# Heads projected in full fp32 with whole output weights, row maxima of two slots in one transpose, and a new order of work within a step, in a two-layer PixArt transformer kernel

## The chip, the cores and the metric

The kernel runs on one core of one Trainium2 chip. The metric is the device time of one execution in microseconds (us); the kernel before stands at 1827.0 us, the median of three runs. The engines of the core are named as the profile names them: PE is TensorE's matmuls and PEld its weight loads, DVE is VectorE, ACT is ScalarE, POOL is GpSimd, SP is SyncE, which here only issues DMAs.

## What is computed

32 sequences of 128 tokens and 256 features pass through two transformer layers in fp32. Both have self-attention, cross-attention against a context of 128 tokens, and an MLP of width 1024, with 16 heads of 16 features. They differ in the modulation, in the gates (layer 0) and in the rotary embedding of queries and keys (layer 1).

```python
# layer 0 (biases left out); layer 1 has rope on q and k, no gates, and a norm before cross-attention too
q, k, v = split(modulate(ln(x)) @ qkv_w)
attn = softmax(q @ k.T * SCALE) @ v             # 16 heads of 16
x = x + gate_sa * (attn @ sa_proj_w)
x = x + cross_attention(ln(x), context) @ ca_proj_w
x = x + gate_ff * (gelu(modulate(ln(x)) @ fc1_w) @ fc2_w)
```

## The kernel before, in words

The 32 sequences are cut into 8 groups of 4 (GB = 4). With two layers there are 16 group passes (groups 0 to 7 are layer 0, groups 8 to 15 layer 1), and each pass has 8 batches: 4 sequences in self-attention (s = SELF), then the same 4 in cross-attention (s = CROSS). All engines run the same written-out schedule. Time is cut into steps; group g starts at step 26 g (PERIOD = 26), self-attention at its step 0, cross-attention at its step 16 (CROSS_FROM), and the MLP of a group is done from its step 36 on (MLP_FROM), that is in steps 10 to 17 of the next group. A step is no fixed time: it is a position in the instruction lists. Tables give the step of each stage (AT_TURN_MAX = 2 means two steps after a batch's first scores), and within a step each engine goes through its stages in a fixed order. Every engine works through its own list in order, and semaphores alone tie the lists together, so a wait at the head of one engine's list holds all that stands behind it.

What a batch passes through, with its place in steps after its start:

- Steps 0 and 1: two rounds of scores on PE (L594), each for two of four row groups, into the two banks `score0` and `score1`. DVE takes the row maxima of each bank with a TENSOR_REDUCE (L1040, `row_max`). The next round may overwrite the banks only when both maxima are made.
- Step 2: PE transposes the maxima (`turn_max`, L639), four 128x128 transposes, and DVE adds them to the transposed queries (`less_max`, L1050), so that the exponent needs no subtraction.
- Steps 3 and 4: the transposed scores (L614), interleaved with the score round of a later batch; ACT takes the exponents (L903, L905).
- Step 6: probabilities times values (`mix_values`, L650); ACT copies the result (L912). Step 7: four transposes back to tokens (`turn_heads`, L658); at step 8 DVE divides by the sum (`scale_heads`, L1056 and L1060) and PE transposes the heads (`turn_back`, L665).
- The heads are then split into a high and a low part for the fp32r product: ACT casts `heads_hi` (L918, step 8), DVE subtracts `heads_lo` (L1065, first in step 9), and PE projects in step 9 (`project`, L488 to L490): six fp32r matmuls of 128x256 for two row tiles, low times high, high times low, high times high. DVE takes the result (L1078 in layer 1, L1082 in layer 0).
- Steps 10 and 11: moments, normalisation (`normalise`, L1005) and the transposes of the normalised rows (`turn_z`, L521), modulated on ACT (L824, L829) into `xt_hi`, with `xt_lo` made on POOL.

The projections of queries, keys and values are called units: twelve fp32r matmuls each into the bank `p_unit`, at the steps of the table UNIT_AT. The projection of the heads uses the same bank. In layer 0, keys leave the bank through ACT (L875, half of the heads) and then DVE (L1012, the other half). In layer 1, queries and keys leave it through ACT (L866), are swapped on DVE (L1025), and rotated on POOL by three products and sums of 1.3 us (L1288, L1291, L1294).

The MLP goes through four hidden tiles at a time (`up`, `down`), six fp32r matmuls each, with the Gelu on ACT and the split of the hidden tile on DVE (L1089, L1091).

## Time and profile before

| what | value |
|---|---|
| median of three runs | 1827.0 us (1824.12 to 1827.39) |
| the profiled execution | 1822.23 us, span 1820.4 us |
| mean granted TensorE clock | 0.967 of full speed |
| PE busy | 1595.2 us, 88% |
| PEld busy | 1390.5 us, 76% |
| DVE busy | 1142.6 us, 63% |
| ACT busy | 970.2 us, 53% |
| POOL busy | 726.6 us, 40% |
| DMA | mean 27 GB/s |

The span is the time from the first to the last recorded instruction on the core; the execution's own time is 1.8 us more. A PE matmul's duration includes its way through the array, and matmuls overlap, so the cost of one in a row of them is the distance from start to start, not its duration. One group period (26 steps) takes 106 to 109 us.

### The profile page before, as it was taken

The numbers are of one execution on the slowest core, as the hardware profiler recorded it, in microseconds if no ns is written. First come the engines' busy times: TensorE is split into PE (matmuls) and PEld (weight loads), VectorE is DVE, ScalarE is ACT, GpSimd is POOL, SyncE is SP. The second block draws the span as 40 slices with busy tenths as digits, with TensorE's granted clock in tenths as the row PEclk, the third lists the DMA queues.
The fourth block names the chain that finished last, engine by engine and source line by source line (L and its number), as shares of the span: only waits on it lengthen the run. The fifth ranks groups of instructions, "written<-read, shape, count | busy, mean of one in ns | idle before, by whom it ended". The sixth has DMA issues, their size and how long they took to land.

```text
span 1820.4 us, 46362 instructions
## 1 busy us (share of the span) xinstructions
PE 1595.2 (88%) x18272; PEld 1390.5 (76%) x18272; DVE 1142.6 (63%) x2630; ACT 970.2 (53%) x2011; POOL 726.6 (40%) x983
## 2 busy tenths in 40 slices
PE   5779989898998989989897898989989898988987
PEld 4657878787887877878787787877878787787866
DVE  3446656566665656657667766666766666676654
ACT  2446455555545656455664545646465564545533
POOL 1332424224142332424536546364454536546321
PEclk9989999999999999999999999999999999999989
DMA  6010010101001010011111100000000000000000
GB/s 218 16 46 2 14 48 14 49 8 43 14 15 48 12 51 3 13 48 33 45 36 30 36 13 25 10 20 12 10 25 13 25 7 19 14 13 13 2 13 13
DMA packets 33972, 49.50 MB, mean 27 GB/s; under 512 B 3456, under 2 KB 24896, under 8 KB 33760
## 3 DMA queue, kind: packets, MB, share of 16 engines
q1 hardware_dynamic: 33760, 46.54, 8.3%
q8 instruction: 149, 2.44, 0.6%
q14 instruction: 63, 0.52, 0.1%
HBM read 38.07 MB, written 8.45 MB: 26 GB/s over the span
## 4 chain that ended last, share of the span: by engine, by line
PE 68%; DVE 14%; issue 8%; ACT 7%; POOL 2%; DMA 0%; SPq 0%; DVEq 0%; ACTq 0%; POOLq 0%
PE score L594 8%; PE p_unit L488 7%; PE score_t L614 7%; PE p_mix L650 5%; PE p_unit L490 5%; PE p_unit L489 5%; DVE neg_max L1040 5%; PE p_out L488 4%; PE p_out L489 3%; PE p_out L490 3%; PE p_turn L639 3%; PE p_turn L665 2%; PE p_turn L658 2%; PE p_mix L521 2%; ACT xt L824 2%
## 5 line engine op out<-in xcount | busy, mean ns | idle before, releaser
L1040 DVE TENSOR_REDUCE neg_max<-score 128x4 f32<-128x512 f32 x512 | 329.9, 687 | 209.8 <-PE score L594 208.9
L594 PE MATMUL score<-k_t,q_t 32*128 32x256 f32 x2048 | 303.1, 415 | 63.9 <-issue 18.3
L614 PE MATMUL score_t<-q_less,k_t 32*128 32x128 f32 x4096 | 313.2, 293 | 0.7 <-ACT probs_t L905 0.7
L594 PEld LDWEIGHTS score<-k_t,q_t 32*128 32x128 f32 x2048 | 192.8, 195 | 111.9 <-issue 56.2
L905 ACT ACTIVATE probs_t<-score_t 128x512 f32<-128x512 f32 x384 | 209.1, 599 | 120.8 <-PE score_t L614 120.6
L614 PEld LDWEIGHTS score_t<-q_less,k_t 32*128 32x128 f32 x4096 | 262.9, 196 | 13.3 <-issue 9.2
L824 ACT ACTIVATE xt<-p_mix,mod_now 128x128 f32<-128x128 f32 x384 | 154.7, 456 | 161.9 <-PE p_mix L521 132.1
L1247 POOL TENSOR_TENSOR xt_lo<-xt,xt_hi 128x256 fp32r<-128x256 f32 x128 | 93.4, 729 | 356.0 <-ACT xt_hi L829 356.0
L488 PE MATMUL p_out<-w_hi,hid_lo 128*128 128x256 f32 x512 | 148.1, 289 | 3.4 <-DVE hid_lo L1091 2.8
L1089 DVE CAST hid_hi<-hid 128x256 fp32r<-128x256 f32 x256 | 94.5, 369 | 83.1 <-ACT hid L891 82.8
L1091 DVE TENSOR_TENSOR hid_lo<-hid,hid_hi 128x256 fp32r<-128x256 f32 x256 | 138.5, 541 | 8.8
L490 PE MATMUL p_out<-w_hi,hid_hi 128*128 128x256 f32 x512 | 143.6, 280 | 0.0
L489 PE MATMUL p_out<-w_lo,hid_hi 128*128 128x256 f32 x512 | 143.4, 280 | 0.0
L650 PE MATMUL p_mix<-probs_t,v_pad 128*32 128x128 f32 x4096 | 139.2, 277 | 1.1 <-ACT xt L824 1.1
L488 PE MATMUL p_unit<-w_hi,heads_lo 128*128 128x256 f32 x256 | 82.8, 323 | 64.9 <-ACT heads_hi L918 33.9
L488 PE MATMUL p_unit<-xt_hi,w_lo 128*128 128x256 f32 x384 | 123.0, 320 | 18.8 <-ACT q_t L870 5.9
L918 ACT CAST heads_hi<-p_turn 128x256 fp32r<-128x256 f32 x128 | 47.6, 372 | 167.3 <-PE p_turn L665 166.7
L891 ACT ACTIVATE hid<-score,bias_cols 128x256 f32<-128x256 f32 x128 | 60.4, 474 | 133.2 <-PE score L490 125.2
L1065 DVE TENSOR_TENSOR heads_lo<-p_turn,heads_hi 128x256 fp32r<-128x256 f32 x128 | 54.2, 423 | 106.1 <-ACT heads_hi L918 106.0
L650 PEld LDWEIGHTS p_mix<-probs_t,v_pad 128*32 128x32 f32 x4096 | 104.6, 110 | 21.1 <-issue 13.1
L1240 POOL TENSOR_TENSOR rstd<-var_eps,minus_half 128x1 f32<-128x1 f32 x192 | 110.2, 574 | 15.0
L488 PEld LDWEIGHTS p_unit<-w_hi,heads_lo 128*128 128x128 f32 x256 | 47.9, 187 | 89.2 <-ACT heads_hi L918 53.1
(151 smaller groups left out, 4525.7 us busy)
## 6 DMA issues: line engine op xcount, KB each, us to landing
ctxt<-in_ctxT SPq DMA_DIRECT2D x16, 512.0 KB, 3.7
side<-gates SPq DMA_DIRECT2D x15, 512.0 KB, 5.6
x_new<-in_x SPq DMA_DIRECT2D x32, 128.0 KB, 2.0
x_mid<-xs SPq DMA_DIRECT2D x8, 512.0 KB, 3.4
x_new<-x_mid SPq DMA_DIRECT2D x32, 128.0 KB, 2.0
out<-xs SPq DMA_DIRECT2D x8, 512.0 KB, 2.9
k_t<-in_L_f_wT SPq DMA_DIRECT2D x2, 1024.0 KB, 5.7
k_t<-in_ln_wT SPq DMA_DIRECT2D x2, 512.0 KB, 7.9
```

The source lines that it names most:

```text
L488: pe.matmul(dst, lhs[1], rhs[0], start=first, stop=False, skip_group_check=shared)
L489: pe.matmul(dst, lhs[0], rhs[1], start=False, stop=False, skip_group_check=shared)
L490: return pe.matmul(dst, lhs[0], rhs[0], start=False, stop=last, skip_group_check=shared)
L594: mm = pe.matmul(score[r % 2][:, t * 2 * N:(t + 1) * 2 * N].rearrange("p (e n) -> p e n", e=2), q_t[s][rows(r), t, tokens], k_t[s][rows(r) ...
L614: mm = pe.matmul(score_t[r % 2][:, x * N:(x + 1) * N], k_t[s][rows(r), t, e, tokens], q_less[rows(r), j % 2, t, e, :], start=True, stop=True)
L650: mm = pe.matmul(p_mix[rows(r), x * N:(x + 1) * N], v_pad[s][:, b, at:at + 32], probs_t[j % 2][:, r, x, :], start=True, stop=True, tile_po ...
L824: op = act.activation(xt[:, k, c, :], p_mix[:, c * P:(c + 1) * P], ACT.Identity, scale=mod_now[k][:, c, b:b + 1], bias=mod_now[k][:, 2 + c ...
L905: op = act.activation(dst, score_t[r % 2][:], ACT.Exp)
L1040: dve.tensor_reduce(by_half[:, :, 2 * r + 1:2 * r + 9:7, 0], score[r % 2][:].rearrange("p (t e n) -> p t e n", t=CT, e=2), AX.X, ALU.max, ...
L1089: dve.tensor_copy(hid_hi[:, u % HID_SLOTS, :], hid[:, u % 2, :]).then_inc(hid_hi_made, 1)
L1091: dve.tensor_tensor(hid_lo[:, u % HID_SLOTS, :], hid[:, u % 2, :], hid_hi[:, u % HID_SLOTS, :].bitcast(F32), ALU.subtract).then_inc(hid_lo ...
L1240: pool.tensor_tensor(rstd[:, k, b:b + 1], var_eps[:, k, b:b + 1], minus_half[:], ALU.pow)\
```

## The change

Four things change.

1. **The heads' projection.** The output weights of self- and cross-attention leave the table of split weights (`w_hi`, `w_lo`) and stand whole in a tile `w_out`, loaded by their own DMAs. ACT copies the transposed heads to `heads_t` in fp32 (one COPY in the place of the cast), the subtraction on DVE (`low_heads`) is gone, and `project` is two fp32 matmuls of 128x256 in the place of six fp32r ones.
2. **Maxima of two slots share one transpose.** The maxima of the two heads of a slot pair are written into one 128-column tile; `turn_max` is two transposes in the place of four, and `less_max` is two SCALAR_TENSOR_TENSOR on 128x256 elements (one for each of the pair, with the column `one_row` as a factor that picks the row) in the place of one TENSOR_TENSOR on 128x512. The two heads of a pair change places in the layout (`by_slot`, `head_mask`, `one_row`).
3. **Tables.** First-norm transposes and units move by a step or two (FIRST_LNT, UNIT_AT), two MLP hidden tiles move between steps, the last `down` stands two steps later.
4. **Order within a step.** On each engine some stages change places.

The core of the diff:

```diff
-FIRST_STATS, FIRST_Z, FIRST_LNT = -13, -11, -10
+FIRST_STATS, FIRST_Z, FIRST_LNT = -13, -9, -9
-UNIT_AT = {-7: ("k", SELF, 0), ...
-           6: ("k", CROSS, 0), 7: ("v", CROSS, 0), 13: ("k", CROSS, 1), 14: ("q", CROSS, 0), 15: ("v", CROSS, 1), 18: ("q", CROSS, 1)}
+UNIT_AT = {-6: ("k", SELF, 0), ...
+           6: ("k", CROSS, 0), 7: ("v", CROSS, 0), 11: ("k", CROSS, 1), 14: ("q", CROSS, 0), 16: ("v", CROSS, 1), 18: ("q", CROSS, 1)}
-for _step, _n in zip(range(MLP_FROM, MLP_FROM + 8), (0, 9, 2, 1, 5, 11, 3, 1)):
+for _step, _n in zip(range(MLP_FROM, MLP_FROM + 10), (0, 10, 1, 1, 6, 12, 1, 0, 0, 1)):
-PE_ORDER = ("round", "proj", "max", "mlp", "norm", "mix", "turn", "first", "unit", "back")
+PE_ORDER = ("round", "proj", "mlp", "max", "mix", "turn", "norm", "first", "unit", "back")
+        w_out = sb("w_out", [P, 2, CT, D])
-        heads_hi = sb("heads_hi", [P, CT, N], F32R)
-        heads_lo = sb("heads_lo", [P, CT, N], F32R)
+        heads_t = sb("heads_t", [P, CT, N])
             def turn_max(group, j):
...
-                for x in range(SLOTS):
-                    mm = pe.transpose(p_turn[:, x * P:(x + 1) * P], neg_max[:, j % 2, x * P:(x + 1) * P], ident[:])
+                for t in range(CT):
+                    mm = pe.transpose(p_turn[:, t * P:(t + 1) * P], neg_max[:, j % 2, t, :], ident[:])
             def project(group, s, b):
...
                 for t in range(CT):
-                    mm = product(p_unit[:, 0:D], (heads_hi[:, t, :], heads_lo[:, t, :]),
-                                 w(W_SA if s == SELF else W_CA, t, D, 0, D), t == 0, t == CT - 1)
+                    mm = pe.matmul(p_unit[:, 0:D], heads_t[:, t, :], w_out[:, s, t, :], start=(t == 0), stop=(t == CT - 1))
-            def high_heads(group, j):
+            def move_heads(group, j):
...
-                act.copy(heads_hi[:].rearrange("p t n -> p (t n)"), p_turn[:, 0:D]).then_inc(heads_hi_made, 1)
+                act.copy(heads_t[:].rearrange("p t n -> p (t n)"), p_turn[:, 0:D]).then_inc(heads_moved, 1)
             def less_max(group, s, b):
...
-                own = q_t[s][:, :, b * N:(b + 1) * N].unsqueeze(2).broadcast_to([P, CT, 2, N])
-                dve.tensor_tensor(q_less[:, j % 2], p_turn[:].rearrange("p (t e n) -> p t e n", t=CT, e=2), own, ALU.add)\
-                   .then_inc(queries_less, 1)
+                for e in range(2):
+                    op = dve.scalar_tensor_tensor(q_less[:, j % 2, :, e, :],
+                                                  p_turn[:, 0:CT * N].rearrange("p (t n) -> p t n", t=CT),
+                                                  one_row[:, e:e + 1], q_t[s][:, :, b * N:(b + 1) * N],
+                                                  ALU.mult, ALU.add)
+                op.then_inc(queries_less, 1)
-            def low_heads(group, j):
-                dve.wait_ge(heads_hi_made, group * 8 + j + 1)
-                dve.tensor_tensor(heads_lo[:].rearrange("p t n -> p (t n)"), p_turn[:, 0:D],
-                                  heads_hi[:].rearrange("p t n -> p (t n)").bitcast(F32), ALU.subtract)\
-                   .then_inc(heads_lo_made, 1)
```

Line numbers in the rows below are those of the kernel before or after, as each list says.

**DVE, group 12 (layer 1), from the end of step 2 to step 3.** Before, from `less_max` of one batch to the result of the projection (L1078):

```order
L1050 TENSOR_TENSOR q_less<-p_turn,q_t 128x512 [waits scored_t,max_turned]
L1025 STREAM_SHUFFLE side<-side 128x512 [waits raw_made]
L1065 TENSOR_TENSOR heads_lo<-p_turn,heads_hi 128x256 [waits heads_hi_made]
L1005 TENSOR_SCALAR z<-xs,mean_var,rstd 128x256 [waits z_turned2,rstd_made2]
L1040 TENSOR_REDUCE neg_max<-score 128x2x2 [waits scored] x2
L1078 TENSOR_TENSOR xs<-p_unit,xs 128x256 [waits projected]
```

And in the changed kernel:

```order
L1055 SCALAR_TENSOR_TENSOR q_less<-p_turn,one_row,q_t 128x2x128 [waits scored_t,max_turned]
L1055 SCALAR_TENSOR_TENSOR q_less<-p_turn,one_row,q_t 128x2x128
L1030 STREAM_SHUFFLE side<-side 128x512 [waits raw_made]
L1010 TENSOR_SCALAR z<-xs,mean_var,rstd 128x256 [waits z_turned2,rstd_made2]
L1045 TENSOR_REDUCE neg_max<-score 128x2x2 [waits scored] x2
L1080 TENSOR_TENSOR xs<-p_unit,xs 128x256 [waits projected]
```

The subtraction that waits for ACT is gone from the head of the step, and the rest keeps its order.

**PE, group 4 (layer 0), from step 20 to step 21.** Before, the transposes of the maxima end step 20, and the round of step 21 (mask, scores, transposed scores) and the unit of the next group's self queries follow:

```order
L639 MATMUL p_turn<-ident,neg_max 128x128 [waits queries_less,max_made]
L639 MATMUL p_turn<-ident,neg_max 128x128 x3
L589 MATMUL score<-mask_row,ones_row 128x512 [waits max_made]
L589 MATMUL score<-mask_row,ones_row 128x512
L594 MATMUL score<-k_t,q_t 128x256 [waits exps_made,queries_less]
L594 MATMUL score<-k_t,q_t 128x256
L614 MATMUL score_t<-q_less,k_t 128x128 x4
L594 MATMUL score<-k_t,q_t 128x256 x2
L614 MATMUL score_t<-q_less,k_t 128x128 x4
L488 MATMUL p_unit<-xt_hi,w_lo 128x256 [waits keys_high,xt_lo_made0,xt_hi_made0]
```

In the changed kernel, from the same transposes on:

```order
L651 MATMUL p_turn<-ident,neg_max 128x128 [waits queries_less,max_made]
L651 MATMUL p_turn<-ident,neg_max 128x128
L533 MATMUL p_mix<-ident,z 128x128 [waits ln_moved0,z_made0]
L533 MATMUL p_mix<-ident,z 128x128
L500 MATMUL p_unit<-xt_hi,w_lo 128x256 [waits queries_made,xt_lo_made0,xt_hi_made0]
L501 MATMUL p_unit<-xt_lo,w_hi 128x256
L502 MATMUL p_unit<-xt_hi,w_hi 128x256
```

Between the transposes and the round of step 21 stand now the last first-norm transpose and the unit of the self keys (12 matmuls), which stood in step 19 before; the unit of the queries keeps its place behind the round, and still waits until the keys have left the bank (`keys_high`). Step 19 gets the last `down` of the MLP, from step 17.

**ACT, group 12 (layer 1), steps 18 and 19.** Before: `modulate` of the third sequence of the next group's first norm (L824 twice, L829) waits for the unit in step 18 (`unit_full`), and the copy of that unit (L866, cross queries) comes behind it:

```order
L882 ACTIVATE k_t<-side,one_row,head_mask 128x2x256 [waits keys_summed]
L824 ACTIVATE xt<-p_mix,mod_now 128x128 [waits unit_full,xt_lo_made0,z_turned0]
L824 ACTIVATE xt<-p_mix,mod_now 128x128
L829 CAST xt_hi<-xt 128x2x128 [waits ln_moved0]
L866 ACTIVATE side<-p_unit 128x512 [waits queries_made,queries_less,unit_full]
L905 ACT_TABLE_LOAD [waits mixed]
```

In the changed kernel:

```order
L833 ACTIVATE xt<-p_mix,mod_now 128x128 [waits xt_lo_made0,z_turned0]
L833 ACTIVATE xt<-p_mix,mod_now 128x128
L838 CAST xt_hi<-xt 128x2x128 [waits ln_moved0]
L875 ACTIVATE side<-p_unit 128x512 [waits queries_made,queries_less,unit_full]
L914 ACT_TABLE_LOAD [waits mixed]
```

The sequence modulated ahead of the copy is now the second one, which doesn't wait for the unit; the third comes behind the exponents of step 19.

## Rows read from the trace of the kernel before

**Rows 1.** The page, busy time of the engines: us, share of the span, instructions

```profile
PE 1595.2 (88%) x18272; PEld 1390.5 (76%) x18272; DVE 1142.6 (63%) x2630; ACT 970.2 (53%) x2011; POOL 726.6 (40%) x983
```

**Rows 2.** The page, the chain that ended last, by engine

```profile
PE 68%; DVE 14%; issue 8%; ACT 7%; POOL 2%; DMA 0%; SPq 0%; DVEq 0%; ACTq 0%; POOLq 0%
```

**Rows 3.** Timeline of PE in group 12, step 3: start, us, what

```profile
1356.38 0.36 PE L488 MATMUL p_unit<-w_hi,heads_lo 128*128 128x256 f32 x1 [0.49 <-ACT v_pad L855]
...
1357.17 0.38 PE L521 MATMUL p_mix<-ident,z 128*128 128x128 f32 x2
1357.38 0.60 PE L658 MATMUL p_turn<-ident,mix_sb 128*128 128x128 f32 x4
1358.41 0.48 PE L594 MATMUL score<-k_t,q_t 32*128 32x256 f32 x2 [0.43 <-DVE neg_max L1040]
```

**Rows 4.** Timeline of PE at the start, the bias products in fp32

```profile
36.69 1.16 PE L794 MATMUL score_t<-probs_t,hid 128*128 128x256 f32 x4
```

**Rows 5.** Line L794, durations of one in ns, least, median and most

```profile
L794 PEld LDWEIGHTS score_t<-probs_t,hid x4: 190/254/337, 36.3 to 37.3; 128*128 128x128 f32 x4
L794 PE MATMUL score_t<-probs_t,hid x4: 379/380/507, 36.7 to 37.5; 128*128 128x256 f32 x4
```

**Rows 6.** Timeline of all engines, group 12, from step 10 to step 11

```profile
1379.71 0.44 PE L665 MATMUL p_turn<-ident,heads 128*128 128x128 f32 x2
1380.19 0.37 ACT L918 CAST heads_hi<-p_turn 128x256 fp32r<-128x256 f32 x1 [0.30 <-PE p_turn L665]
...
1380.59 0.42 DVE L1065 TENSOR_TENSOR heads_lo<-p_turn,heads_hi 128x256 fp32r<-128x256 f32 x1 [1.06 <-ACT heads_hi L918]
...
1381.12 0.36 PE L488 MATMUL p_unit<-w_hi,heads_lo 128*128 128x256 f32 x1 [0.97 <-ACT heads_hi L918]
```

**Rows 7.** Waits of PE's weight loads: us in total, times, longest

```profile
PEld p_unit L488 <- ACT heads_hi L918: 53.1, 43, 1.5
PEld score L594 <- DVE neg_max L1040: 36.4, 48, 3.6
```

**Rows 8.** Timeline of DVE in group 12, step 3

```profile
1355.23 0.42 DVE L1065 TENSOR_TENSOR heads_lo<-p_turn,heads_hi 128x256 fp32r<-128x256 f32 x1 [1.29 <-ACT heads_hi L918]
1355.57 1.28 DVE L1005 TENSOR_SCALAR z<-xs,mean_var,rstd 128x256 f32<-128x256 f32 x1
1356.78 1.28 DVE L1040 TENSOR_REDUCE neg_max<-score 128x4 f32<-128x512 f32 x2
```

**Rows 9.** Timeline of all engines in group 4 (layer 0), step 20

```profile
560.27 0.99 DVE L1012 TENSOR_SCALAR k_t<-p_unit,head_mask,key_bias 128x256 f32<-128x256 f32 x2 [4.26 <-ACT k_t L875]
561.18 1.28 DVE L1040 TENSOR_REDUCE neg_max<-score 128x4 f32<-128x512 f32 x2
...
562.52 0.58 PE L589 MATMUL score<-mask_row,ones_row 32*128 32x512 bf16 x2 [2.43 <-DVE neg_max L1040]
```

**Rows 10.** Timeline of all engines in group 12 (layer 1), steps 19 and 20

```profile
1425.24 0.81 ACT L824 ACTIVATE xt<-p_mix,mod_now 128x128 f32<-128x128 f32 x2 [1.42 <-PE p_unit L490]
...
1426.38 0.59 ACT L866 ACTIVATE side<-p_unit 128x512 f32<-128x512 f32 x1
...
1427.24 1.30 POOL L1288 TENSOR_TENSOR q_t<-side,cos_t 128x512 f32<-128x512 f32 x1
...
1431.38 0.48 PE L594 MATMUL score<-k_t,q_t 32*128 32x256 f32 x2 [2.60 <-issue]
```

**Rows 11.** Windows of groups 11 and 12: stretch, engines' busy time, PEclk

```profile
1236.60:1343.00 106.40, 94.81 (x1133) 83.13 (x1132) 73.04 (x168) 59.10 (x123) 53.71 (x66) 1.00 0.05 16
1343.00:1451.50 108.50, 97.10 (x1130) 85.22 (x1130) 72.75 (x168) 59.10 (x123) 53.64 (x66) 0.97 0.05 16
```

**Rows 12.** Line L1050 (less_max), durations of one in ns

```profile
L1050 DVE TENSOR_TENSOR q_less<-p_turn,q_t x128: 681/682/692, 59.9 to 1769.4; 128x512 f32<-128x512 f32 x128
```

**Rows 13.** Line L1005 (normalise) in group 12, durations of one in ns

```profile
L1005 DVE TENSOR_SCALAR z<-xs,mean_var,rstd x8: 403/407/1281, 1346.3 to 1417.1; 128x256 f32<-128x256 f32 x8
```

**Rows 14.** Window of one period of layer 0, group 2, as in rows 11

```profile
253.70:362.50 108.80, 98.87 (x1144) 85.83 (x1141) 66.60 (x157) 60.30 (x127) 35.16 (x57) 0.97 0.09 26
```

More of the change, by code:

```diff
@@ L258, in build_blocks @@
                  k_t[1][:].rearrange("p t e n -> p (t e n)")]
+        stage = [spare[c][:, 0:CHUNKS[c + 1] - CHUNKS[c]] for c in range(4)]
+        new_stage = [spare[c % 2 * 3][:, 0:CHUNKS[c + 1] - CHUNKS[c]] for c in range(4)]
         ada = [xs[:].rearrange("p a b c -> p (a b c)")[:, 0:6 * D],
@@ L469, in body @@
                             load_weights(1, CHUNK_AT[group, step], new_stage, w_new)
+                        if (group, step) in HEADS_OUT_AT:
+                            s = HEADS_OUT_AT[group, step]
+                            sp.wait_ge(projected, NG * 8 - 4 if s == SELF else NG * 8)
+                            load_heads_out(1, s)
                         if step == LAST:
@@ L753, in body @@
                             turn_heads(group, 4 * s + b)
+                    for group, step in live(t):
+                        for s, b in batch_at(step, AT_LNT):
+                            turn_z(group, s + 1, b)
                     for group, step in live(t):
@@ L953, in body @@
                     for group, step in live(t):
+                        if layer_of(group) == 1 and step in KEYS_AT:
+                            low_keys(group, KEYS_AT[step])
+                    for group, step in live(t):
+                        for n in GELU_AT.get(step, ()):
+                            gelu(group, n)
+                    for group, step in live(t):
                         for s, b, h in round_at(step, AT_EXP):
@@ L969, in body @@
                     for group, step in live(t):
-                        if layer_of(group) == 1 and step in KEYS_AT:
-                            low_keys(group, KEYS_AT[step])
+                        for s, b in batch_at(step, AT_MIX + ACT_MIX):
+                            move_mix(group, 4 * s + b)
                     for group, step in live(t):
@@ L1140, in body @@
                     for group, step in live(t):
-                        for s, b in batch_at(step, AT_TURN_BACK + DVE_LOW):
-                            low_heads(group, 4 * s + b)
+                        for k, b in normed_at(step, AT_Z, FIRST_Z):
+                            normalise(group, k, b)
                     for group, step in live(t):
@@ L1148, in body @@
                             moments(group, k, b)
-                    for group, step in live(t):
-                        for k, b in normed_at(step, AT_Z, FIRST_Z):
-                            normalise(group, k, b)
                     for group, step in live(t):
@@ L1159, in body @@
                     for group, step in live(t):
-                        for s, b in batch_at(step, AT_TURN_MAX):
-                            less_max(group, s, b)
-                    for group, step in live(t):
-                        if layer_of(group) == 1 and UNIT_AT.get(step - DVE_SWAP, "v")[0] != "v":
-                            swap(group, UNIT_AT[step - DVE_SWAP])
-                    for group, step in live(t):
                         for s, b in batch_at(step, AT_PROJ + DVE_OUT):
@@ L1170, in body @@
                             high_keys(group, KEYS_AT[step])
+                    for group, step in live(t):
+                        for s, b in batch_at(step, AT_TURN_MAX):
+                            less_max(group, s, b)
                     for group, step in live(t):
@@ L1178, in body @@
                             make_masks(group)
+                    for group, step in live(t):
+                        if layer_of(group) == 1 and UNIT_AT.get(step - DVE_SWAP, "v")[0] != "v":
+                            swap(group, UNIT_AT[step - DVE_SWAP])
                     for group, step in live(t):
@@ L1314, in body @@
                     for group, step in live(t):
+                        for s, b in batch_at(step, AT_PROJ + DVE_OUT):
+                            if layer_of(group) == 0:
+                                add_output(group, 4 * s + b)
+                    for group, step in live(t):
                         for k, b in normed_at(step, AT_LNT + ACT_MOD, FIRST_LNT + ACT_MOD):
```

149 lines of the change are left out of this document (67 added, 82 removed).

## Prediction

> **What bounds the kernel now.** I read the busy times first: PE is at work 88% of the span, DVE 63%, ACT 53%, POOL 40% [rows 1]. The chain that ended last says the same of the path: 68% of it is PE, DVE has 14%, ACT 7%, and 8% is issue [rows 2]. So work taken from PE should count nearly in full, except in steps whose length is set by a wait. I then read the timeline of two layer-1 steps and one of layer 0 for those waits. Three kinds matter.
>
> First, in steps 11, 13 and 15 nothing stands between the transpose of the heads and their projection: PE transposes at 1379.71, ACT casts at 1380.19, DVE subtracts at 1380.59, and PE begins at 1381.12 [rows 6]. PE's weight loads wait 53.1 us in all for this, 43 times [rows 7].
>
> Second, a score round may start only when both maxima of the round before are made. Rounds wait 36.4 us for that [rows 7]. In step 3 of group 12 the round waits until 1358.41 [rows 3], since on DVE `heads_lo` had waited for ACT with everything behind it, then `normalise` took 1.28 us, and the maxima began only at 1356.78 [rows 8].
>
> Third, the joints around step 20. In layer 0 the self keys leave their bank through ACT and then DVE ahead of the maxima, and the next round stands idle for 2.43 us [rows 9]. In layer 1 the rotation of the last cross queries is late: ACT copies them at 1426.38, POOL starts at 1427.24, and the round that needs them starts at 1431.38 after 2.60 us of idling [rows 10].
>
> **The change part by part.** The sum is made against the profiled execution, 1822.2 us, which is 4.8 us under the median. There are 128 batches and 16 group passes.
>
> *Projection.* Six fp32r matmuls take 0.79 us from the first start to the next stage (1356.38 to 1357.17) [rows 3], 0.13 us each. Two fp32 matmuls of 128x256 are seen at the start: four of them take 1.16 us to the end of the last, which itself lasts 0.38, so three distances make 0.78 us, 0.26 each [rows 4, 5]. The longest of them lasts 507 ns against 379, so it ran in part at the lower clock; if the whole first distance was doubled, d = 0.78/4 = 0.195. I take 0.22, between. A projection is then 0.44 us, and saves 0.35: 128 x 0.35 = 45 us (34 with 0.26, 51 with 0.195).
>
> The weight side could speak against this. The fp32 load of 128 columns has 190 ns as its least duration [rows 5], and it is inside the distance above, so no further price is due. The Trainium skill, TensorE: Matmul & The Clock Gate, in the section on Fast Weight Load, says that the fast load is on for 128 weights only where the type is not FP32; by that rule heads and weights kept in full precision would lose it, and this trace shows no separate price of that. What it would make is the second rival.
>
> *Transposes.* Four transposes last 0.60 us and two 0.38 [rows 3]: two fewer are 0.22 us. 128 x 0.22 = 28 us, hidden nowhere, since PE is the engine at work; in a step that waits anyway it is worth nothing.
>
> *The subtraction on DVE, as a link.* From its start at 1380.59 to PE's start at 1381.12 is 0.53 us; without it PE could start about 0.1 us after ACT's end at 1380.56, 0.45 us sooner [rows 6]. Three places a group: 48 x 0.45 = 22 us (0 if something else is late, 27 from the whole distance and more in step 15).
>
> *The subtraction on DVE, as a block.* In steps 1, 3 and 5 it stood ahead of `normalise` and the maxima. What is won is bounded by the 36.4 us of rounds that wait for maxima [rows 7], part of which stays at step 20. In step 3 of group 12 the projection would still begin at 1356.38, since it waits there for ACT's `v_pad`; with 0.44 for it, and 0.22 and 0.44 for the transposes behind it, the round could start at 1357.5 in place of 1358.41 [rows 3], 0.9 us, of which 0.35 is counted. I take half of the bound, 18 us (0 to 36).
>
> *Step 20, layer 0.* One first-norm transpose pair and the unit of the self keys (twelve matmuls of 0.12 us) now fill the wait of 2.43 us. But the same keys leave the bank one step later: what takes from 560.27 to the maxima's end [rows 9] now stands ahead of the maxima of step 21, beside that step's round. The wait moves and shrinks; I take 1.2 us x 8 = 10 us (0 to 19).
>
> *Steps 19 and 20, layer 1.* The copy of the cross queries no longer stands behind `modulate`, which starts at 1425.24, as the copy could; at most 1.14 us [rows 10]. The swap on DVE still stands behind two maxima, so I take 0.6 x 8 = 5 us. The last `down` (six matmuls, 0.7 us) moves from step 17 into this wait of 2.60 us and so is free: 6 us. Together 11 (0 to 15).
>
> *Clock.* One period of layer 1 at a granted clock of 1.00 takes 106.4 us and the next, at 0.97, 108.5 [rows 11]; a stretch at 1.2 GHz in a period thus costs 2.1 us. Layer 0 has it too, 0.97 [rows 14], behind the long idling of step 20. That idling shrinks in layer 0 (I take half of 8 x 2.1, 8 us) and may lengthen in layer 1, which loses up to 4 x 2.1 (I take 4). Net 4 us (-8 to 17).
>
> *less_max.* Two operations on 128x256 elements, of which the nearest row is `heads_lo`: it reads the same two memories, lasts 0.42 us and lets the next start 0.34 later [rows 8]. Twice 0.34 to 0.42 stands against one of 0.68 [rows 12]: 0 to 0.16 us more, 20 us in all at most. Behind the transposes PE has other work in nearly every step (values, a unit), which covers it; where the cover is gone the next round is late by the whole of it. I take 3 us.
>
> *Covered at nothing:* ACT's copy in place of its cast (same size), the smaller weight splits at the change of layers, two more DMAs of the output weights on SP's queue, which wait for projections long done, and the store two steps later, which the next write to its tile follows by four steps.
>
> Sum: 45 + 28 + 22 + 18 + 10 + 11 + 4 - 3 = 135 us. Not all of it adds up, because a shorter PE step meets DVE, whose even steps hold division, moments, maxima and `less_max`. I hold back 10 us for these new waits: 125. 1822.2 - 125 = 1697, and 1702 at the level of the median.
>
> **The rivals.**
>
> *Only the work counts (15%).* DVE and ACT keep the pace in the rounds, so the second kind of wait and the joints stay, and a quarter of the saved PE work falls into waits: 0.75 x 73 + 11 for half of the link = 66 us, giving 1761. For it: 14% of the chain is DVE's [rows 2]. Against it: DVE loses an operation of 0.42 us a batch and stands idle 1.29 us ahead of the very one that is removed [rows 8].
>
> *The fp32 product is dearer in place (6%).* If each of its two loads stays exposed, 2 x 0.19 us come on top [rows 5], and the projection takes 0.82: nothing is saved on it, 45 us less, 1747. This is the case that the skill's rule on fast loads would make; the distance of rows 4, which holds four loads, speaks against it.
>
> *Everything adds up (14%).* No holding back, all joints at their upper bounds and no stretch at 1.2 GHz in layer 0: 125 + 10 + 9 + 4 + 13 + 5 = 166 us, 1661.
>
> *Slower (4%).* `less_max` might be held by POOL as `normalise` is: that one lasts 407 ns in the median and 1281 at most [rows 13], 0.87 more. 256 halves at 0.87 are 223 us, and the change loses from 144 held halves on (125/0.87); all of them held gives 1702 + 223 = 1925. Against it: L1050, with the same operands, never lasts over 692 ns in 128 [rows 12]. The Trainium skill, SBUF — State Buffer, section Who interferes with whom, says that a DVE instruction with at most one SBUF input outside the two-port modes does not contend with GpSimd; by that rule, and `q_t` is the one tensor here from SBUF, the trace of L1050 agrees.
>
> **How the numbers follow.** The forecast has 61%, with its own range of 1675 to 1735. 1650 to 1765 takes in both neighbours and the dearer product, and leaves out the slower case and what lies beyond: under 2 in 10. About 0.2% (4 us) is what a measurement here can tell from no change. Faster by more: 0.61 + 0.15 + 0.06 + 0.14 = 0.96, of which I move 0.02 to no change, for the first rival carried on until the waits take all; slower 0.04.
>
> **What would show it.** In the profile after: 256 fp32 matmuls into `p_unit` about 0.22 us apart; three projections a group that wait under 0.8 us for ACT; no DVE row ahead of `normalise` that waits for ACT; the wait ahead of layer 0's round of step 21 gone and a smaller one in step 21 on `keys_high`; PE's busy time down by some 70 us; periods of about 100 us in layer 0 and layer 1. I am wrong if PE's idle time grows by as much as its work falls, if the rounds wait more for maxima than 36 us, or if the granted clock falls below 0.96.

## The result, and the profile after

The changed kernel takes 1799.2 us (median of 4 runs, 1797.4 to 1803.8) against 1825.6 (4 runs, 1823.4 to 1827.4) for the kernel before on the same chip: ratio 0.986, 95% interval 0.9836 to 0.9884. It is faster, by 26 us; the forecast was 125 us, and the time lies far above its range of 1650 to 1765. The profiled execution took 1797.4 us with a mean granted clock of 0.959 (0.967 before).

The page of the changed kernel (busy time, then the chain that ended last):

```profile
PE 1594.9 (89%) x17760; PEld 1372.3 (76%) x17760; DVE 1117.6 (62%) x2628; ACT 972.2 (54%) x2009; POOL 720.3 (40%) x983
...
PE 74%; DVE 8%; ACT 8%; issue 6%; POOL 3%; DMA 1%; SPq 0%; DVEq 0%; ACTq 0%; POOLq 0%
```

This is already half of the answer. PE was to lose some 70 us of work and lost 0.3 us [rows 1]. Its share of the chain grew from 68 to 74% while DVE's fell from 14 to 8% [rows 2]: waits for DVE were taken out, but PE's own work did not shrink. The count of matmul records shows why. Before to after, 768 fp32r products go, 256 transposes go, and 256 fp32 products come: 768 fewer. The page has 512 fewer. Line L687, the new projection, in the view of one line (durations in ns, least, median, most):

```profile
L687 PEld LDWEIGHTS p_unit<-w_out,heads_t x512: 186/190/337, 87.5 to 1760.2; 128*128 128x128 f32 x171
L687 PE MATMUL p_unit<-w_out,heads_t x512: 379/379/765, 87.5 to 1760.4; 128*128 128x256 f32 x171
```

256 instructions are 512 records: each fp32 product is recorded as two matmuls, and each of them has its own weight load. The four records of [rows 4] that priced it were two instructions (the line of the bias products issues four in all, and the trace of before has eight records of it). Group 12, step 3, timeline of PE, the place of [rows 3]:

```profile
1339.20 1.10 PE L687 MATMUL p_unit<-w_out,heads_t 128*128 128x256 f32 x4 [0.49 <-ACT v_pad L864]
1340.13 0.60 PE L670 MATMUL p_turn<-ident,mix_sb 128*128 128x128 f32 x4
1340.57 0.38 PE L533 MATMUL p_mix<-ident,z 128*128 128x128 f32 x2
1340.88 0.48 PE L606 MATMUL score<-k_t,q_t 32*128 32x256 f32 x2
```

The projection takes 0.93 us to the start of the next stage, where the six split products took 0.79. The round starts 1.68 us behind the projection's start; before, it was 2.03, of which 0.43 was idling for `neg_max`. That idling is gone, and 0.14 of the gain is paid to the product. What was right in kind: the link without the subtraction, here from step 10 to step 11 of group 12 (all engines; [rows 6] before):

```profile
1362.21 0.44 PE L677 MATMUL p_turn<-ident,heads 128*128 128x128 f32 x2
1362.68 0.37 ACT L927 COPY heads_t<-p_turn 128x256 f32<-128x256 f32 x1 [0.30 <-PE p_turn L677]
1363.11 1.13 PE L687 MATMUL p_unit<-w_out,heads_t 128*128 128x256 f32 x4 [0.46 <-ACT heads_t L927]
```

From transpose to product it is now 0.90 us, before 1.41: 0.51 less, as forecast (0.45).

The waits of PE and of its weight loads (us in total, times, longest):

```profile
PEld p_unit L687 <- ACT heads_t L927: 47.2, 51, 1.7
PEld score L606 <- DVE neg_max L1045: 29.8, 42, 2.3
PE p_unit L500 <- DVE k_t L1017: 18.5, 16, 2.3
PE score L606 <- POOL q_t L1293: 30.8, 8, 4.3
PE p_turn L677 <- DVE q_less L1055: 12.7, 22, 0.9
```

The last two have grown. The rotated queries keep one round of each layer-1 period waiting, 30.8 us in all; the same eight rounds waited 25.0 us before (2.59 or 2.60 us in six of them, as in [rows 10]). And the transposes that turn the heads back wait for `less_max` 22 times, 12.7 us, where they waited 8 times, 2.2 us: both use `p_turn`, and `less_max` has become longer. Its line, and the place in group 12 on PE (maxima turned, last product of the values, then the wait):

```profile
L1055 DVE SCALAR_TENSOR_TENSOR q_less<-p_turn,one_row,q_t x256: 463/475/485, 63.6 to 1745.0; 128x256 f32<-128x256 f32 x128
```

```profile
1341.99 0.44 PE L651 MATMUL p_turn<-ident,neg_max 128*128 128x128 f32 x2
...
1343.57 0.28 PE L502 MATMUL p_unit<-w_hi,xt_hi 128*128 128x256 f32 x1
1344.29 0.41 PE L677 MATMUL p_turn<-ident,heads 128*128 128x128 f32 x2 [0.44 <-DVE q_less L1055]
```

Steps 18 to 20 of a layer-1 period, all engines:

```profile
1403.97 0.56 PE L500 MATMUL p_unit<-xt_hi,w_lo 128*128 128x256 f32 x1
...
1406.77 0.60 ACT L875 ACTIVATE side<-p_unit 128x512 f32<-128x512 f32 x1 [1.17 <-PE p_unit L502]
...
1407.44 1.28 POOL L1287 TENSOR_TENSOR q_t<-side,cos_t 128x512 f32<-128x512 f32 x1 [1.03 <-ACT side L875]
...
1407.83 1.29 DVE L1045 TENSOR_REDUCE neg_max<-score 128x4 f32<-128x512 f32 x2 [2.13 <-PE score L606]
...
1409.04 0.72 DVE L1030 STREAM_SHUFFLE side<-side 128x512 f32<-128x512 f32 x1
...
1411.25 1.26 POOL L1293 TENSOR_TENSOR q_t<-q_t,side 128x512 f32<-128x512 f32 x1
...
1412.72 0.48 PE L606 MATMUL score<-k_t,q_t 32*128 32x256 f32 x2 [3.76 <-POOL q_t L1293]
```

ACT copies the unit at once, as forecast, and POOL starts at once. But the shuffle on DVE stands behind two maxima and ends at 1409.76, and the rest of the rotation on POOL follows from that. The round waits 3.76 us where it waited 2.60 [rows 10]. The unit ahead of it, from 1403.97, has products 0.21 us apart where 0.12 is usual. The windows say why (one period each, from about step 3 of groups 3, 10, 11 and 12; then the unit's stretch alone; the last columns are PEclk, DMA share, GB/s):

```profile
370.30:476.10 105.80, 96.83 (x1114) 83.17 (x1113) 66.55 (x158) 60.52 (x127) 34.88 (x57) 0.98 0.09 27
1122.30:1228.50 106.20, 97.12 (x1098) 84.08 (x1098) 71.56 (x168) 59.39 (x123) 53.61 (x65) 0.97 0.06 17
1228.50:1336.90 108.40, 99.42 (x1099) 86.24 (x1098) 70.61 (x168) 59.38 (x123) 53.47 (x65) 0.94 0.05 16
1336.90:1443.00 106.10, 97.16 (x1099) 84.45 (x1098) 70.63 (x168) 59.44 (x123) 53.53 (x65) 0.97 0.05 17
1402.10:1406.70 4.60, 4.60 (x29) 4.02 (x28) 2.40 (x5) 2.42 (x6) 2.19 (x3) 0.63 0.00 0
```

Most of that stretch ran at 1.2 GHz, one of the clock's two levels. No period of layer 1 shown here is free of it, where group 11 was before, at 1.00 and 106.4 us [rows 11]. A period of layer 0 is 105.8 us, 3 us shorter [rows 14]; these three of layer 1 are 106.9 on average, against 107.5 for the two of [rows 11].

### The profile page after: what moved, and what is told of

The parts are those of the page before. It is cut to its first block, busy times and chain, and to the rows that moved or that the text cites. A ratio compares the mean times of both kernels' runs of the same rounds, so it can differ in the third digit from the quotient of the medians.

```text
span 1795.6 us, 45329 instructions
## 1 busy us (share of the span) xinstructions
PE 1594.9 (89%) x17760; PEld 1372.3 (76%) x17760; DVE 1117.6 (62%) x2628; ACT 972.2 (54%) x2009; POOL 720.3 (40%) x983
## 4 chain that ended last, share of the span: by engine, by line
PE 74%; DVE 8%; ACT 8%; issue 6%; POOL 3%; DMA 1%; SPq 0%; DVEq 0%; ACTq 0%; POOLq 0%
PE score L606 9%; PE p_unit L687 8%; PE score_t L626 7%; PE p_unit L500 6%; PE p_mix L662 5%; PE p_unit L501 5%; PE p_unit L502 5%; PE p_out L500 3%; PE p_out L502 3%; PE p_out L501 3%; DVE neg_max L1045 3%; PE p_turn L670 2%; PE p_mix L533 2%; PE p_turn L677 2%; PE p_turn L651 2%
## 5 line engine op out<-in xcount | busy, mean ns | idle before, releaser
L606 PE MATMUL score<-k_t,q_t 32*128 32x256 f32 x2048 | 303.9, 416 | 65.5 <-POOL q_t L1293 30.8
L626 PE MATMUL score_t<-q_less,k_t 32*128 32x128 f32 x4096 | 307.0, 289 | 0.8 <-ACT probs_t L914 0.8
L626 PEld LDWEIGHTS score_t<-q_less,k_t 32*128 32x128 f32 x4096 | 257.1, 192 | 13.3 <-issue 9.2
L914 ACT ACTIVATE probs_t<-score_t 128x512 f32<-128x512 f32 x384 | 209.1, 598 | 106.2 <-PE score_t L626 105.8
L687 PE MATMUL p_unit<-w_out,heads_t 128*128 128x256 f32 x512 | 144.3, 404 | 42.8 <-ACT heads_t L927 15.8
L1091 DVE CAST hid_hi<-hid 128x256 fp32r<-128x256 f32 x256 | 102.0, 398 | 81.6 <-ACT hid L900 80.8
L500 PE MATMUL p_out<-w_hi,hid_lo 128*128 128x256 f32 x512 | 149.1, 291 | 1.5 <-DVE hid_lo L1093 0.3
L687 PEld LDWEIGHTS p_unit<-w_out,heads_t 128*128 128x128 f32 x512 | 87.2, 190 | 75.1 <-ACT heads_t L927 47.2
L500 PE MATMUL p_unit<-xt_hi,w_lo 128*128 128x256 f32 x384 | 126.1, 328 | 20.6 <-DVE k_t L1017 15.6
L927 ACT COPY heads_t<-p_turn 128x256 f32<-128x256 f32 x128 | 47.7, 372 | 154.5 <-PE p_turn L677 154.1
L1055 DVE SCALAR_TENSOR_TENSOR q_less<-p_turn,one_row,q_t 128x256 f32<-128x256 f32 x256 | 111.2, 476 | 28.2 <-PE p_turn L651 28.2
L501 PE MATMUL p_unit<-xt_lo,w_hi 128*128 128x256 f32 x384 | 117.6, 306 | 0.0
```

Of the source, the lines that this page charges most:

```text
L500: pe.matmul(dst, lhs[1], rhs[0], start=first, stop=False, skip_group_check=shared)
L501: pe.matmul(dst, lhs[0], rhs[1], start=False, stop=False, skip_group_check=shared)
L606: mm = pe.matmul(score[r % 2][:, t * 2 * N:(t + 1) * 2 * N].rearrange("p (e n) -> p e n", e=2), q_t[s][rows(r), t, tokens], k_t[s][rows(r) ...
L626: mm = pe.matmul(score_t[r % 2][:, x * N:(x + 1) * N], k_t[s][rows(r), t, e, tokens], q_less[rows(r), j % 2, t, e, :], start=True, stop=True)
L687: mm = pe.matmul(p_unit[:, 0:D], heads_t[:, t, :], w_out[:, s, t, :], start=(t == 0), stop=(t == CT - 1))
L914: op = act.activation(dst, score_t[r % 2][:], ACT.Exp)
```

## The experiments

Each kernel was timed against the kernel before on the same chip. "Busy" kernels have filler: superfluous transposes of the identity into an unused quarter of a bank, at places where PE waits. They change no result.

### One part alone: projection, maxima, order

e1 is the kernel before with part 1 of the change alone, e2 with part 2 alone, e3 with parts 3 and 4 alone; e4 is the changed kernel with the split projection put back, that is parts 2 to 4. Their diffs are the pieces shown under the change. The kernel before had medians of 1822.9 to 1825.6 us in the different series of runs, so a difference between two kernels of different series is uncertain by a few us; the ratios are each within one series.

> The kernel before with the projection alone changed (whole fp32 weights, two fp32 matmuls for six fp32r, no subtraction on DVE). Theory 1: an fp32 product of 128x256 is worked as two passes of 0.216 us, so a projection costs 0.97 us in place of 0.79 (128 x 0.18 = 23 us lost), and the link without DVE gives back some 16 to 25 us: ratio 0.995 to 1.005. Theory 2 (the product costs 0.44 us as forecast, and new waits eat the gain elsewhere): the projection's own distance to the next stage is 0.44 us and the ratio is 0.98 or lower.

> The kernel before with the shared transposes of the maxima alone. Theory 1: 0.22 us less PE work in each of 128 batches counts nearly in full, 20 to 28 us, ratio 0.985 to 0.989. Theory 2 (waits of the rounds for DVE take it): under 8 us, ratio over 0.995.

> The kernel before with the new tables and the new order within a step alone. Theory 1: the joints around step 20 gain 1 to 2 us in a period of layer 0 and about nothing in layer 1, start-up loses some: 5 to 15 us, ratio 0.992 to 0.997. Theory 2 (the new order moves waits into worse places): slower, ratio 1.002 to 1.01.

> The changed kernel with the projection put back as it was (six fp32r matmuls, subtraction on DVE). Theory 1: the projection part was worth about nothing, so this is within 5 us of the changed kernel, 1795 to 1805. Theory 2 (the projection part is the gain): over 1815.

| kernel | us | ratio, interval | clock |
|---|---|---|---|
| e1 projection alone | 1817.4 | 0.9961, 0.9949 to 0.9973 | 0.966 |
| e2 maxima alone | 1835.7 | 1.0068, 1.0056 to 1.0080 | 0.955 |
| e3 order alone | 1802.5 | 0.9894, 0.9878 to 0.9911 | 0.963 |
| e4 maxima and order | 1799.1 | 0.9868, 0.9854 to 0.9882 | 0.960 |
| all (the change) | 1799.2 | 0.9860, 0.9836 to 0.9884 | 0.959 |

The projection, my largest term, is worth 7 us alone and nothing beside the other parts (e4 and the change are equal). The shared maxima, with 28 us less of transposes, make the kernel 12 us slower alone. The parts don't add up: 0.7% slower and 1.1% faster together give 1.3% faster. Theory 1 held for e1 and e4. e2 was expected by neither of its theories to be slower than the kernel before (theory 2, a ratio over 0.995, is the nearer), and e3 gains more than its theory 1 gave. e2's windows in layer 1 show a part of the reason, a granted clock of 0.95 in each of three periods (one is shown), where the kernel before has 0.97 and 1.00 in turn [rows 11]; the wait for `less_max` grew too, to 37.4 us in all from 11.9 in the kernel before (PE's waits of e2):

```profile
1146.80:1255.90 109.10, 96.89 (x1114) 84.67 (x1113) 73.66 (x175) 59.06 (x123) 53.66 (x66) 0.95 0.05 16
```

```profile
PE score L594 <- DVE q_less L1050: 24.3, 31, 1.8
PE p_turn L665 <- DVE q_less L1050: 13.1, 21, 0.9
```

### The price of the fp32 product

e5 leaves out one of the two products of each projection, so the second half of every head row is missing from the attention's output. That puts the price where the forecast had it.

```diff
-                for t in range(CT):
-                    mm = pe.matmul(p_unit[:, 0:D], heads_t[:, t, :], w_out[:, s, t, :], start=(t == 0), stop=(t == CT - 1))
+                mm = pe.matmul(p_unit[:, 0:D], heads_t[:, 0, :], w_out[:, s, 0, :], start=True, stop=True)
```

> The changed kernel with one of the two fp32 matmuls of each projection left out (half of the contraction is not summed), so that a projection costs about the 0.44 us that was forecast for both. Theory 1 (the price of the product was the wrong term, and work taken from PE counts): 0.53 us x 128 = 68 us at most, some 40 to 65 us under the changed kernel, ratio to before 0.95 to 0.965. Theory 2 (waits, or stretches at 1.2 GHz, take what is saved): under 20 us, ratio over 0.975.

Measured: 1753.3 us, ratio 0.9612 (0.9595 to 0.9629), 46 us under the changed kernel. In the timeline of e5 one product is two records and 0.51 us to the next stage:

```profile
1307.14 0.67 PE L686 MATMUL p_unit<-w_out,heads_t 128*128 128x256 f32 x2
1307.65 0.38 PE L533 MATMUL p_mix<-ident,z 128*128 128x128 f32 x2
```

0.93 less 0.51 is 0.42 us, 128 of which are 54 us, and 46 arrive. That is theory 1, and more than four fifths of the work taken. But part of it is the clock's: the four runs have 0.960 to 0.973, those of the changed kernel 0.952 to 0.959. With the clock held (e13 below) 34 of the 54 us arrive, some 63%.

### The clock, held up by filler

e6 is the changed kernel with filler: 8 transposes in step 14 and 8 in step 17 of each group, 24 in step 19 of layer 1, 14 in step 21 of layer 0. e7 is e2 and e8 the kernel before with filler in their own waits (steps 14, 17, 19 and 20).

```diff
+            def busy(bank, n):
+                for _ in range(n):
+                    pe.transpose(bank[:, 3 * P:4 * P], ident[:], ident[:])
...
+                        if step == 19 and layer_of(group) == 1:
+                            pe.wait_ge(queries_less, group * 8 + 5)
+                            busy(p_turn, 24)
```

> The changed kernel with idle PE time filled: 8 transposes of the unit matrix into a free part of a bank in step 14, 8 in step 17, 24 in step 19 (layer 1) and 14 in step 21 (layer 0), all inside waits seen in the trace. Theory 1 (idle stretches make the granted clock fall and each fall costs about 2 us): clock from 0.959 to 0.98 or more, 15 to 30 us faster than the changed kernel. Theory 2 (the clock falls for another reason or costs nothing, since other engines set these steps): clock unchanged, same time or 5 to 10 us slower by the added work.

> The kernel with the shared transposes alone (12 us slower than before) with filling transposes in steps 14, 17, 19 (layer 1, 16 of them) and 20. Theory 1 (it was slower only because the clock fell in every period): clock 0.98 or more and under 1805 us, and 15 to 28 us under the kernel before with the same filling. Theory 2 (less_max in two operations holds the path): no faster than the kernel before with the same filling.

> The kernel before with the same filling as in the run ahead of this one. Theory 1: clock 0.98 or more, 10 to 25 us faster than before. Theory 2: same or slower.

Measured: e6 1769.2 us, ratio 0.9698 (0.9680 to 0.9715), clock 0.984; e7 1793.1, 0.9831 (0.9813 to 0.9849), clock 0.981; e8 1800.6, 0.9866 (0.9847 to 0.9886), clock 0.985. 70 us of added PE work take 30 us off the changed kernel and 24 off the kernel before. Theory 1 held for e6 and e8. For e7 it held in clock and time, but e7 is only 7.6 us under e8, not 15 to 28. A layer-0 and a layer-1 period of e6, its step 18 of group 12 (4.58 us without filler, at a clock of 0.63, about the last window of the list above), and the filler's rows:

```profile
362.80:467.20 104.40, 98.92 (x1144) 85.38 (x1144) 66.64 (x157) 60.35 (x127) 34.70 (x57) 1.00 0.10 28
1211.60:1315.10 103.50, 98.57 (x1138) 85.94 (x1137) 70.98 (x169) 59.12 (x123) 53.70 (x65) 1.00 0.06 17
1380.09:1383.43 3.34, 3.16 (x25) 2.60 (x25) 2.17 (x5) 2.26 (x6) 1.46 (x2) 1.00 0.00 0
```

```profile
L682 PE MATMUL p_turn<-ident 128*128 128x128 f32 x432 | 52.8, 274 | 0.0
L682 PE MATMUL p_mix<-ident 128*128 128x128 f32 x128 | 17.3, 281 | 0.0
```

Where the 30 us come from can be read from the lengths of the steps. A step's length is here the distance from the start of its score round to that of the next (steps 7 to 15 and 23 to 25 have no further round and are one distance each), as the median of groups 1 to 6 in layer 0 and 9 to 14 in layer 1. From the changed kernel to e6, step 18 is 1.53 us shorter in layer 0, steps 18 and 20 are 1.27 and 1.37 shorter in layer 1, and no other differs by more than 0.1. These are the steps behind the waits that the filler fills; nothing in them was changed. So it is the clock, and no shorter wait, that gives the time back.

### The parts once more, with the clock held

e9 is e4 with e6's filler, e10 is e3 with it.

> The kernel after with the projection made as before (split heads, six fp32r products) and the same filler transposes as in e6. Theory 1: the projection in full precision costs as much TensorE time as the six split products and its shorter way from turned heads to product is used up by waits elsewhere, so with the clock held the two projections are equal: 1766 to 1773 us, within 0.2% of e6 (1769.2). Theory 2: the link that it takes out (0.5 us at steps 11 and 13, 32 to 64 times) is worth something once the clock does not fall: e9 is 8 to 25 us dearer than e6, 1777 to 1794 us.

> Only the new order of work on the kernel before, with the filler transposes. Theory 1: the parts add up when the clock is held: before with filler is 1800.6, the shared maxima gave 7.6 us there, the projection about 0, so the order is worth the rest: 1769 + 8 = 1777 us (1773 to 1781). Theory 2: the order and the shared maxima need each other (the maxima leave room that only the new order uses): e10 is above 1785 us.

Measured: e9 1768.9 us, ratio 0.9696 (0.9678 to 0.9715); e10 1777.3, 0.9738 (0.9722 to 0.9755). Theory 1 held for both. At a held clock the parts do add up, as far as they were tried: from e8 the order gives 23.3 us (e10), the shared maxima 8.4 on top (e9; 7.6 without the order, e7), the projection nothing (e6 is 0.3 us above e9). The filler of e8 and e7 stands in other steps than that of e10, e9 and e6; in each of the five traces at least 11 of the 16 periods have no stretch at 1.2 GHz. e9 and e6 are, with e11 below, the fastest versions found that compute the whole reference.

The order's 23.3 us do not all lie where the forecast had them. By the lengths of the steps from e8 to e10, steps 17 to 21 are 1.5 us shorter in layer 0 and 0.8 in layer 1, 19 us over sixteen periods. Another 11 us come from steps 7 to 15 of layer 1, here as windows of group 11, first e8, then e10; no term of the forecast was for them, and which of the edits does it was not tried apart:

```profile
1242.49:1288.37 45.88, 42.88 (x454) 39.93 (x453) 31.09 (x79) 23.52 (x50) 20.15 (x26) 1.00 0.04 13
```

```profile
1232.18:1276.70 44.52, 42.40 (x453) 39.73 (x452) 31.51 (x79) 23.39 (x48) 19.90 (x26) 1.00 0.05 14
```

Steps 16 and 23 to 25 give some 5 more. These are 35 us, and 23 arrive. The other 12 are lost at the start and around the change of layers: the first score round starts at 52.6 us in place of 48.7, and the first period of layer 1 takes 117.7 us in place of 113.2.

### The second operation of less_max

e12 is e6 with a third such operation, of the same shape, whose result nothing reads.

```diff
+                dve.scalar_tensor_tensor(spare_less[:], p_turn[:, 0:CT * N].rearrange("p (t n) -> p t n", t=CT),
+                                         one_row[:, 0:1], q_t[s][:, :, b * N:(b + 1) * N],
+                                         ALU.mult, ALU.add).then_inc(spare_made, 1)
```

> e6 with a third, superfluous operation of the same shape (128x256, one_row times maxima plus queries) ahead of the two that write the lowered queries; its result is not read. It prices one such operation: 64 places, 0.39 us each. Theory 1: the operation is on the chain only where a score round or the turned-back heads wait for it (steps 4, 22 to 24, two to three places of eight a period): 16 to 24 places a layer, 12 to 20 us dearer than e6, 1781 to 1789 us, so that the second operation, which the change adds, costs about that too. Theory 2: it is on the chain everywhere, 64 x 0.39 = 25 us, 1794 us. Theory 3: it lies beside TensorE's work, under 4 us.

Measured: 1801.8 us, ratio 0.9876 (0.9855 to 0.9897), 32.6 us above e6, more than any theory gave. The expectation miscounted: there are 128 such places, not 64, so "everywhere" is 50 us, and 65% of it counts. PE's waits for `less_max`, first in e12, then in e6, e7 and e8:

```profile
PE p_turn L679 <- DVE q_less L1081: 32.3, 47, 1.3
PE score L608 <- DVE q_less L1081: 18.5, 25, 2.2
```

```profile
PE p_turn L677 <- DVE q_less L1074: 12.5, 22, 0.8
PE score L606 <- DVE q_less L1074: 10.4, 16, 1.8
```

```profile
PE score L594 <- DVE q_less L1068: 16.9, 29, 1.5
PE p_turn L665 <- DVE q_less L1068: 13.9, 22, 0.8
```

```profile
PE score L594 <- DVE q_less L1068: 2.4, 8, 0.9
PE p_turn L665 <- DVE q_less L1068: 2.2, 8, 0.5
```

The wait is 4.6 us in the kernel before with filler, 30.8 with the shared maxima, 22.9 with the new order too (e6), and 50.8 with the third operation. Nearly all of it is new with part 2 of the change. e12's own filler waits for `less_max` too, in steps 19 and 21, but the loss is not there: from e6 to e12, steps 4, 18, 20 and 22 of layer 1 are 0.39 us longer each, steps 7 to 15 and 23 to 25 too, and steps 19 and 21 are the same; in layer 0, 19 and 21 are 0.37 and 0.29 shorter.

The same view prices the shared maxima. From e8 to e7, steps 2, 6 and 18 of layer 0 are 0.21 or 0.22 us shorter, which is the price of two transposes, and steps 4, 20, 22 and 23 to 25 are 0.18 or 0.19 longer: 0.39 for the second operation less 0.21. The sum over a period of layer 0 is nothing, in layer 1 it is 0.8 us. Step 4 of group 3, first e8, then e7:

```profile
371.70:375.48 3.78, 3.53 (x44) 3.07 (x43) 3.00 (x7) 1.97 (x5) 2.11 (x4) 1.00 0.02 4
```

```profile
371.15:375.11 3.96, 3.31 (x41) 2.85 (x41) 3.19 (x8) 1.97 (x5) 2.11 (x4) 1.00 0.00 0
```

### The shuffle ahead of the maxima

e11 is e6 with the shuffle of the queries' rotation issued ahead of `row_max` on DVE.

```diff
+                        if layer_of(group) == 1 and UNIT_AT.get(step - DVE_SWAP, "v")[0] == "q":
+                            swap(group, UNIT_AT[step - DVE_SWAP])
```

> e6 with one more edit: in layer 1 the shuffle of the queries' rotation is issued on VectorE ahead of the two maxima of its step instead of behind them. Theory 1: the score round of step 20 in layer 1 waits for the rotation (4.3 us at the longest), whose shuffle stands behind two maxima of 1 us each; ahead of them it comes about 1 us earlier, 8 periods, 7 to 12 us less than e6: 1757 to 1762 us. Theory 2: the maxima are then late and the next score round waits for its bank instead: 1767 to 1772 us, as e6, or dearer.

Measured: 1768.0 us, ratio 0.9687 (0.9669 to 0.9705): no difference to e6 that can be told. The joint itself went as theory 1 said. The rounds of steps 19 and 20 in e6, then in e11:

```profile
1383.43 0.48 PE L606 MATMUL score<-k_t,q_t 32*128 32x256 f32 x2 [0.18 <-issue]
...
1389.52 0.48 PE L606 MATMUL score<-k_t,q_t 32*128 32x256 f32 x2 [1.18 <-issue]
```

```profile
1385.07 0.48 PE L606 MATMUL score<-k_t,q_t 32*128 32x256 f32 x2 [0.18 <-issue]
...
1390.17 0.48 PE L606 MATMUL score<-k_t,q_t 32*128 32x256 f32 x2 [0.20 <-issue]
```

The step is 5.10 us in place of 6.09. It is given back within the period: over the layer-1 periods the median distance from the round of step 22 to the next is 3.97 us in e11 and 3.34 in e6, and steps 10 to 15 are 0.2 longer. In those steps too the queries' shuffle now stands ahead of maxima; that this is the cause was not tried apart.

### Product price and clock at once

e13 is e5 with e6's filler, and leaves out the same half of the projection.

> e5 with the filler transposes of e6: each projection is one fp32 product of 128 columns of the heads instead of two, so the second half of every head row is left out of the attention's output. It puts TensorE's price of a projection at about the 0.44 us that the prediction took, with the clock held. Theory 1: the dear product and the clock are two causes that add up: e6 (1769.2) less the 46 us that leaving the product out took from the kernel after, 1720 to 1730 us. Theory 2: they are one cause seen twice (the shorter projection already shifted the low-clock stretches, its clock was 0.962 though, or the filler ends up behind the shorter projection): 1735 to 1750 us.

Measured: 1734.8 us, ratio 0.9516 (0.9503 to 0.9529), at the edge of theory 2, between the two. With the clock held, one dear product in each projection costs 34 us, not 46: the other 12 us of e5's gain do not come on top of the clock's. e13 is 64 us under the changed kernel. These are not 64 of the 97 us between forecast and measurement, though: filler takes 24 us off the kernel before as well, from which the forecast was counted.

## Why the prediction was wrong

The direction was right, and the likeliest case failed by its first term. The table sets the terms beside what the busy kernels measured, since only there do the parts add up.

| term | forecast | measured |
|---|---|---|
| projection and its link | 45 + 22 | 0 (e9 to e6) |
| transposes, block of maxima, less_max | 28 + 18 - 3 | 8 (e10 to e9) |
| tables and order, forecast for steps 19 to 21 | 10 + 11 | 23 (e8 to e10) |
| clock | 4 | -5 (filler gives 30.0 us after, 24.9 before, as differences of the medians) |
| held back | -10 | |
| sum | 125 | 26 |

**The step that failed: the price of the fp32 product.** "A projection is then 0.44 us" rested on four records of [rows 4, 5], read as four instructions. They were two, so the distance of 0.26 or 0.22 us was that of half a product. The projection takes 0.93 us in the place of 0.79; 128 x 0.14 is 18 us lost where 45 were to be won. The link is shorter by 0.51 us, as forecast, and about pays this back: the sum is nothing. The reader can catch this in the trace of before: rows of a line are to be counted against the instructions of the code before a distance between them is used. The second rival, a projection of 0.82 us, was the right case in size, with 6%; its mechanism, exposed weight loads, was not: the loads last 190 ns in L687 as in [rows 5] and lie beside the products, and what is doubled is the number of matmul records. The Trainium skill, FP8 and Floating Point Precision, section TensorE Precision Notes, says that a true fp32 product makes four passes through the array. An estimate by that rule, with an fp32r product as one pass, is 8 times the distance of an fp32r product, here 0.119 us (seven of them in the rows below, from 1336.27 to 1337.10): 0.95 us. The trace agrees in time, with 0.93, though it records each fp32 product as two matmuls, 0.22 us apart, and not as four. With 0.93 in its place my sum gives 63 us less (128 x 0.49), 1765 us. The largest other part of the miss is the maxima's, 43 us forecast and 8 measured.

```profile
1336.27 0.28 PE L501 MATMUL p_unit<-w_lo,xt_hi 128*128 128x256 f32 x1
...
1337.10 0.28 PE L502 MATMUL p_unit<-w_hi,xt_hi 128*128 128x256 f32 x1
```

**Transposes and less_max.** Two transposes fewer are worth 0.21 us, as forecast, but only in steps that do not wait for `less_max`. "Behind the transposes PE has other work in nearly every step (values, a unit), which covers it" failed. The two operations start 0.39 us apart and last 0.47, 0.86 in place of 0.68, a little past my upper bound of 0.16 us more. What waits is not only the next score round: turning back the heads uses the same bank, which I had not looked up in the list of the bank's users. Where PE waits, the gain of 0.21 turns into a loss of 0.18, so that layer 0 gets nothing and the whole is 8 us.

**The block of maxima.** 18 us were expected from the wait for `neg_max`; it fell from 36.4 to 29.8 us on the weight loads. The gain needed the shorter projection too, and the step that it was read from got it only in part (0.43 us in step 3, less the 0.14 of the product).

**Steps 19 to 21.** 21 us forecast, 23 measured at a held clock, and this agreement is partly luck: steps 17 to 21 gave 19 (12 in layer 0, forecast 10; 7 in layer 1, forecast 11), and the 16 from other steps and the 12 lost at the start and at the change of layers were in no term. In layer 0 the wait moved to `keys_high`, as said: 1.9 us a period, 13 of the 18.5 us of L500's wait for `k_t`. In layer 1 the copy came earlier, the shuffle stayed behind the maxima, and the wait grew, since the `down` and the shorter steps ahead of it only moved PE's arrival forward.

**The clock.** I forecast a small gain, on half of a layer's stretches at 1.2 GHz gone. The mean granted clock fell instead, from 0.967 to 0.959, below the 0.96 that I had named as a sign of being wrong; at two levels that is about 147 us at 1.2 GHz in place of 120. The stretches moved: they fall now in step 18, after 0.99 us of idling for `modulate`, and in layer 1 also after the wait of 3.76 us ahead of the round of step 20. In layer 0 they did get shorter (0.98 in the period shown, before 0.97). Layer 1 lost its free periods, and the first 150 us of the span have a clock of 0.83 where they had 0.90. What filler gives back is 30 us in the changed kernel and 24 in the kernel before.

**Held back.** The flat 10 us had no row behind them. The new waits that the runs show are those for `less_max` (30.8 us with filler in e7, 4.6 in e8), and they are counted above, in the maxima.

## What to carry to other kernels

Before a duration or a distance is taken from a trace, count its rows against the instructions in the code: an fp32 matmul is two rows there, and two of them cost 0.93 us here where the six fp32r products that split them cost 0.79. When an operation on a shared bank is lengthened, list everyone who takes that bank next, not only who reads the result. When a term comes out right, look whether it does so in the steps that it was made for. When PE's waits are moved about, look where the stretches at 1.2 GHz will fall, and try filler in the longest waits before other tuning: it gave 30 us here, where the whole change gave 26.

## What was not expected of the hardware

An fp32 product of 128x256 is recorded as two matmuls about 0.22 us apart, with a weight load of 190 ns each. Filler of 70 us in PE's waits raised the mean granted clock from 0.959 to 0.984 and took 30 us off; with it every period shown has 1.00. A SCALAR_TENSOR_TENSOR of 128x256 from PSUM and SBUF lasts 475 ns and lets the next start after 0.39 us, against 0.42 and 0.34 for the TENSOR_TENSOR of the same size [rows 8].
